# Quantised rows turned by transposing DMA transfers instead of TensorE

## What is computed

```
x = layernorm(x + attention(x, Wq, Wk, Wv, Wo))      # 16 heads of 64, 8 kv heads, rope, tanh cap, causal
scale = max(absmax(x, -1), 1e-7) / 127
q = clip(round(x / scale), -128, 127)                # int8
acc = einsum("bsk,nk->bsn", q, weight)               # the sum in whole numbers
y = float16(acc * scale * w_scale + bias)
out = layernorm(x + y)
```

## Time and profile before

| | |
|---|---|
| median of the three runs | 1320.56 us |
| profiled execution, in all | 1322.9 us |
| its span, first to last instruction | 1321.2 us |
| TensorE busy | 1272.4 us, 96% |
| VectorE busy | 1038.7 us, 79% |
| ScalarE busy | 901.4 us, 68% |
| GpSimd busy | 377.7 us, 29% |
| mean granted TensorE clock | 0.989 |
| DMA, mean rate | 145 GB/s |

### The profile page before, as it was taken

The page is one execution under the profiler, slowest core; times in us unless marked ns, Lnnn a source line. Parts: engine busy times, 40 slices in busy tenths (PEclk is TensorE's granted clock), DMA queues, the critical chain, the costliest instruction groups (busy, mean ns, idle before and its releaser), DMA issues.

```text
span 1321.2 us, 17006 instructions
## 1 busy us (share of the span) xinstructions
PE 1272.4 (96%) x5840; PEld 936.2 (71%) x5840; DVE 1038.7 (79%) x1314; ACT 901.4 (68%) x1019; POOL 377.7 (29%) x438
## 2 busy tenths in 40 slices
PE   6899999999999999999999999999999999999896
PEld 5677777767766777677776777767777677777573
DVE  3588988983679888896478988898556988888566
ACT  4278787862677777875368867687447777879464
POOL 4232231111751111111383111111147211112165
PEclk9899999999999999999999999999999999999898
DMA  9683736495724464748551654466762355353551
GB/s 317 140 280 101 175 113 168 119 243 152 189 69 107 113 149 99 203 92 244 159 152 65 152 112 124 96 184 182 206 185 80 93 139 110 104 116 119 148 142 56
DMA packets 112401, 191.44 MB, mean 145 GB/s; under 512 B 19382, under 2 KB 65980, under 8 KB 104764
## 3 DMA queue, kind: packets, MB, share of 16 engines
q1 hardware_dynamic: 107564, 179.88, 52.1%
q10 hardware_dynamic: 4752, 10.49, 2.1%
HBM read 84.67 MB, written 38.54 MB: 93 GB/s over the span
## 4 chain that ended last, share of the span: by engine, by line
PE 83%; DVE 7%; issue 3%; ACT 3%; DMA 2%; POOL 1%; SPq 1%; POOLq 0%; DVEq 0%; ACTq 0%
PE ps L829 27%; PE ps L749 19%; PE ps L803 17%; PE ps L873 11%; PE ps L770 6%; PE ps L893 1%; PE ps L849 1%; DVE prob_lo L1292 1%; DVE prob_hi L1288 1%; DMA div<-y_scratch 1%; DVE xT L1208 1%; DVE stats L1370 1%; ACT probs L1032 1%; ACT probs L1027 0%; PE ps L883 0%
## 5 line engine op out<-in xcount | busy, mean ns | idle before, releaser
L829 PE MATMUL ps<-prob_hi,v 128*65 128x512 f32 (+3 forms) x1280 | 410.7, 371 | 8.4 <-DVE prob_lo L1292 8.4
L1027 ACT ACTIVATE probs<-ps 128x1024 f32<-128x1024 f32 x288 | 293.6, 1019 | 133.3 <-PE ps L803 133.3
L1292 DVE TENSOR_TENSOR prob_lo<-probs,prob_hi 128x1024 fp32r<-128x1024 f32 x288 | 360.0, 1250 | 9.8
L1535 POOL TENSOR_SCALAR_AFFINE_SELECT probs<-probs 128x256 f32<-128x256 f32 (+1 forms) x192 | 155.6, 818 | 705.3 <-ACT probs L1032 705.3
L803 PE MATMUL ps<-qk 128*128 128x512 f32 (+1 forms) x1280 | 314.5, 372 | 3.0 <-issue 1.8
L1032 ACT ACTIVATE probs<-probs 128x1024 f32<-128x1024 f32 x288 | 305.7, 1061 | 8.6
L749 PE MATMUL ps<-xT,w_ring 128*128 128x512 f32 x1152 | 286.9, 393 | 4.3 <-issue 4.3
L803 PEld LDWEIGHTS ps<-qk 128*128 128x128 f32 x1280 | 224.6, 189 | 62.6 <-issue 3.8
L1288 DVE CAST prob_hi<-probs 128x1024 fp32r<-128x1024 f32 x285 | 203.9, 715 | 79.7 <-POOL probs L1535 48.1
L749 PEld LDWEIGHTS ps<-xT,w_ring 128*128 128x128 f32 x1152 | 215.7, 189 | 50.9 <-issue 5.8
L829 PEld LDWEIGHTS ps<-prob_hi,v 128*65 128x65 f32 (+1 forms) x1280 | 170.7, 135 | 98.7 <-DVE prob_lo L1292 14.6
(11 more groups left out here) (92 smaller groups left out, 964.1 us busy)
## 6 DMA issues: line engine op xcount, KB each, us to landing
qk<-work_r SPq DMA_DIRECT2D x64, 512.0 KB, 8.8
qk<-work_r SPq DMA_DIRECT2D x256, 128.0 KB, 2.7
y_scratch<-sums SPq DMA_DIRECT2D x128, 130.0 KB
y_raw<-y_scratch SPq DMA_DIRECT2D x64, 256.0 KB, 4.3
wo<-wo_scratch SPq DMA_DIRECT2D x7, 2048.0 KB, 8.7
w_ring<-w_scratch SPq DMA_DIRECT2D x12, 1024.0 KB, 6.9
x_raw<-X_T SPq DMA_DIRECT2D x16, 512.0 KB, 6.7
x_in<-X SPq DMA_DIRECT2D x32, 256.0 KB, 4.3
```

The lines of the kernel that those rows point to most:

```text
L829: mm = nc.tensor.matmul(sums_ps[:, :, GQ - w:GQ], v[:, kt, v0:v0 + width], p[:, at, col:col + REP * w].rearrange("p (h q) -> p h q", h=REP ...
L1027: nc.scalar.activation(probs[:, prob_place(g), :], scores[:, g % 2, :], ACT.Tanh, scale=SCORE_SCALE / SOFTCAP).then_inc(capped, 1)
L1292: nc.vector.tensor_tensor(prob_lo[:, prob_place(g), :], probs[:, prob_place(g), :], prob_hi[:, hi_place(g), :].bitcast(F32), ALU.subtract) ...
L1535: nc.gpsimd.affine_select(out=diag, in_=diag, compare_op=ALU.is_ge, fill=0.0, base=0, pattern=[[0, n], [1, P]], channel_multiplier=-1).the ...
```

## The change

The four transposes by the identity on TensorE, the bank they wrote and ScalarE's copy of that bank are gone, with `ident16`. In their place ScalarE issues, right behind the write of `q16`, four DMA transfers that transpose 128 x 128 values of two bytes each from `q16` into `q16T`, of which there are now two, taken in turn, each with its own semaphore. Before issuing, ScalarE waits for its own write, and from tile 2 on for the matmul that read the same `q16T` last. `linear` waits for the four transfers of its tile and, for tile 0, for the copies of the sums that lie in its banks. `quantise` waits for the transfers of the tile before. TensorE's queue has `linear` of tiles 6 and 7 at the same places between the next batch's projections as before.

```diff
-        q16T = over("q16T", "prob_hi", [P, KC, P], BF16, skip=6 * C)
+        q16T = [over("q16T0", "prob_hi", [P, KC, P], BF16, skip=6 * C),
+                over("q16T1", "prob_hi", [P, KC, P], BF16, skip=4 * T + 6 * C)]
...
-        ident16 = sb("ident16", [P, P], BF16)
...
-        q16_ps = ps[:, PV_BANK, 0:C // 2].bitcast(BF16)
...
+        def turned_upto(b, t):
+            return 64 * (b * NT // 2 + t // 2 + 1)
...
@@ TensorE, weigh
-                    if first and (j, c) == (0, 0) and b >= 1:
-                        pe.wait_ge(qT_ready, rows_upto(b - 1, NT - 1))
...
-            def turn_q(b, t):
-                pe.wait_ge(q_done, rows_upto(b, t))
-                if t == 0:
-                    pe.wait_ge(sums_kept, groups_upto(b, NKV - 1, G - 1))
-                for k in range(KC):
-                    mm = nc.tensor.transpose(q16_ps[:, k * P:(k + 1) * P], q16[:, k * P:(k + 1) * P], ident16[:, :])
-                mm.then_inc(q_turned, 1)
-
             def linear(b, t):
-                pe.wait_ge(qT_ready, rows_upto(b, t))
+                pe.wait_ge(q_turned[t % 2], turned_upto(b, t))
                 if t == 0:
                     pe.wait_ge(ffn_cast, 1)
+                    pe.wait_ge(sums_kept, groups_upto(b, NKV - 1, G - 1))
...
-                    mm = nc.tensor.matmul(ffn_ps(b, t), q16T[:, k, :], ffn_wT[:, k, :], start=(k == 0), stop=(k == KC - 1))
+                    mm = nc.tensor.matmul(ffn_ps(b, t), q16T[t % 2][:, k, :], ffn_wT[:, k, :], start=(k == 0), stop=(k == KC - 1))
...
                         linear(b, t - 2)
-                    if t >= 1:
-                        turn_q(b, t - 1)
...
                 if more:
-                    project(m, 0, 8, 20)
-                turn_q(b, NT - 1)
-                if more:
-                    project(m, 0, 20, 24)
+                    project(m, 0, 8, 24)
                 linear(b, NT - 1)
...
@@ ScalarE
                 if t >= 1:
-                    act.wait_ge(q_turned, rows_upto(b, t - 1))
+                    act.wait_ge(q_turned[(t - 1) % 2], turned_upto(b, t - 1))
...
-            def keep_q(b, t):
-                act.wait_ge(q_turned, rows_upto(b, t))
-                nc.scalar.activation(q16T[:, :, :].rearrange("p k n -> p (k n)"), q16_ps, ACT.Copy).then_inc(qT_ready, 1)
+
+            def turn_q(b, t):
+                act.wait_ge(q_done, rows_upto(b, t))
+                if t >= 2:
+                    act.wait_ge(acc_done, rows_upto(b, t - 2))
+                for k in range(KC):
+                    act.dma_start(q16T[t % 2][:, k, :], q16[:, k * P:(k + 1) * P],
+                                  transpose=True).then_inc(q_turned[t % 2], 16)
...
-                    if t >= 2:
-                        keep_q(b, t - 2)
...
                     quantise(b, t - 1)
+                    turn_q(b, t - 1)
                 if more:
                     exponent(b + 1, 0)
-                keep_q(b, NT - 2)
...
                 quantise(b, NT - 1)
+                turn_q(b, NT - 1)
                 if more:
                     cap(b + 1, 1)
                     norm2(b, NT - 3)
-                    keep_q(b, NT - 1)
...
@@ GpSimd, at the start
-            nc.gpsimd.memset(ident16[:, :], 0.0).then_inc(const_zero, 1)
...
-            for i in (ident, ident16):
-                nc.gpsimd.affine_select(out=i[:, :], in_=i[:, :], compare_op=ALU.not_equal, fill=1.0, base=0,
-                                        pattern=[[-1, P]], channel_multiplier=1).then_inc(const_made, 1)
+            nc.gpsimd.affine_select(out=ident[:, :], in_=ident[:, :], compare_op=ALU.not_equal, fill=1.0, base=0,
+                                    pattern=[[-1, P]], channel_multiplier=1).then_inc(const_made, 1)
```

More of the change, by code:

```diff
@@ L283, in attention_block @@
         q_done = sem("q_done")
-        q_turned = sem("q_turned")
-        qT_ready = sem("qT_ready")
+        q_turned = [sem(f"q_turned{n}") for n in range(2)]
         acc_done = sem("acc_done")
@@ L775, in turn_tables @@
             def turn_tables():
-                pe.wait_ge(const_made, 3)
+                pe.wait_ge(const_made, 2)
                 pe.wait_ge(tables_spread, 1)
@@ L1392, in _ @@
             nc.vector.tensor_copy(spread[0:REP, :], spread_f32[0:REP, :]).then_inc(spread_set, 1)
-            dve.wait_ge(const_made, 3)
+            dve.wait_ge(const_made, 2)
             nc.vector.tensor_copy(v[:, :, 0:V_LO].rearrange("p t (j e) -> p t j e", e=VJ)[:, :, :, ONE:VJ],
@@ L1567, in _ @@
             nc.gpsimd.memset(ident[:, :], 0.0).then_inc(const_zero, 1)
-            nc.gpsimd.memset(ident16[:, :], 0.0).then_inc(const_zero, 1)
             nc.gpsimd.memset(one[:, :], 1.0).then_inc(const_made, 1)
             nc.gpsimd.memset(spread_f32[0:REP, :], 1.0).then_inc(const_zero, 1)
-            pool.wait_ge(const_zero, 5)
-            for i in (ident, ident16):
-                nc.gpsimd.affine_select(out=i[:, :], in_=i[:, :], compare_op=ALU.not_equal, fill=1.0, base=0,
-                                        pattern=[[-1, P]], channel_multiplier=1).then_inc(const_made, 1)
+            pool.wait_ge(const_zero, 4)
+            nc.gpsimd.affine_select(out=ident[:, :], in_=ident[:, :], compare_op=ALU.not_equal, fill=1.0, base=0,
+                                    pattern=[[-1, P]], channel_multiplier=1).then_inc(const_made, 1)
             nc.gpsimd.affine_select(out=spread_f32[0:REP, :], in_=spread_f32[0:REP, :], compare_op=ALU.is_ge, fill=0.0,
```

## The result

The changed kernel takes 1424.57 us (median of three runs, 1419.3 to 1426.43) against 1320.56 before: 1.077 times, 95% interval 1.073 to 1.081, slower. The forecast was 1335, range 1315 to 1380; its direction was right and its size was not. The profiled execution is the shortest of the three, 1419.3 us, with a span of 1417.5, against 1321.2 before.

A forecast was written before the change was run, and what follows sets the result against it. TensorE, busy 96% of the span, was taken as the bound. 8.3 us at three seam ends, 1.05 in the last seam and 5.1 for the clock made +14.4, 1337.3 on the profiled execution, so 1335 us; range 1315 to 1380.

The forecast's parts named there:

- I = 0.60: Time for ScalarE to issue one transposing DMA, taken as 0.60 us, with ends 0.338 and 1.222.
- rival B: ScalarE becomes the bound in the seams: 1355 us at 0.80 per issue, 1398 at 1.222; chance 0.17.
- H: Hold of ScalarE's queue per tile, the wait for the write plus four issues: 2.45 us, ends 1.4 and 4.9.
- T: Time from a tile's quantised write until all four transfers have landed: 4.55 us, ends 3.1 and 6.4.
- clock 1.7: Loss to TensorE's lowered clock after its stall at a seam's end: 1.7 us for each of three seams, +5.1.
- its landing is hidden too: In a seam's middle the landing costs nothing, as `linear` wants the row more than a tile later.
- most of the gain: Removing TensorE's transposes gains 1.95 us per seam: five times 0.31 plus 0.40 at tile 0.
- the path through the seam's end: Tile 6's hold passes through exponent, mask, inverse deviation, norm1 and quantise to tile 7; net +2.77 us per seam, +8.3 for three.
- The gap of about 5 us: TensorE stands idle about 5.3 us before tile 7's `linear` in three seams.
- C of the prediction: The four transposes don't overlap, each landing 2.1 us after the one before: 1351 us; chance 0.13.
- D: Short issues and landings, and VectorE catching up during the stall behind the seams, make the kernel faster: 1313 us; chance 0.22.
- E: The transfers go as element-sized pieces and not as a hardware transpose: far over 1400 us; chance 0.03.

The follow-up runs named there:

- alone: A kernel that computes nothing and makes transposing and plain DMAs of several sizes on an idle core; 1.10 us per issue for 128 columns.
- plain_aside: The kernel before, plus four plain 128x128 DMAs per tile on ScalarE into a buffer nobody reads; 1361.91 us, 1.031 times.
- sp_four: The changed kernel with its four transposing DMAs per tile issued by SyncE, behind its loads, in place of ScalarE; 1378.4 us, 1.0425 times.
- one_dma: The changed kernel with one transposing DMA of 128x512 per tile in place of four of 128x128; 1336.46 us, 1.0115 times.
- late_weights: The changed kernel with SyncE's two weight loads of a seam moved from row tile 1 to row tile 4; 1417.32 us, 1.072 times.
- one_late_exp: As one_late, with tile 6's transposing DMA issued behind the next batch's first exponent in place of ahead of it; 1315.34 us, 0.9954 times.
- one_late: As one_dma, with SyncE's two weight loads of a seam issued at row tile 4 in place of 1; 1327.81 us, 1.0051 times.
- late_after: As one_late, with SyncE's 512 KB load for the next batch waiting until tile 7 has landed transposed; 1321.85 us, 0.9992 times.

## Why the prediction missed

**The step that failed is the length of one issue.** It took I = 0.60 from SyncE's plain puts of 128 KB, "nearest" since a transpose writes many short pieces. The pieces are short, as the page of after shows (39862 DMA packets under 512 B, 19382 before), but the length of the issue doesn't follow from them. A transposing DMA takes 1.265 in the kernel and 1.10 with nothing else running, a plain one 0.47 (128x512, alone) to 0.62 (128x128, plain_aside). The upper end, 1.222 from the 512 KB puts, agrees with the measured length by accident: a transposing DMA is that long with 4 KB as with 128 (16x128 and 128x512 in alone). The ends were kept, but the range was cut at 1380, inside rival B.

**It was rival B.** "From I = 0.64 on, round and hold pass 7.11 and each tile of a seam pays": shown by the round of 9.31 us, where 6.95 was forecast, by sp_four and one_dma. B had a chance of 0.17 and a price of 1398 at I = 1.222. With the measured sizes its sum is: middle 5 x (9.30 - 7.42) = 9.4 a seam; end, with H = 0.05 + 4 x 1.265 = 5.11 and T = 0.05 + 3 x 1.265 + 2.6 = 6.45, 5.11 + 6.45 - 2.28 = 9.3; clock 1.7; together 20.4 three times, and 9.4 + 6.45 - 1.36 = 14.5 in the last: +76.

**What the sum had at nothing.** Measured are +96 on the span. The missing 20 are about 7 in each of three seams and 4.4 in the last, less the 3.8 us of scatter ahead of the first seam and about 1 between seams. The 7 are as large as the waits for the late first landing (8.2, 6.9 and 6.7 us): "so there its landing is hidden too" was said of the middle and taken for the first tile as well, and `quantise`'s wait for the transfers of the tile before, 12.6 us in three waits, had no term at all. The first tile's transposes hold ScalarE's queue from 330.1, SyncE's loads for the seam are issued from 332.6 to 334.7, and the DMA engines are full. In the first seam they land 5.3 to 9.9 us after their issue, those of tiles 4 to 6 2.2 to 2.9, and tile 7's 2.2 to 4.5. First the changed kernel, then the kernel before at the place of the same loads (columns as in the earlier trace rows):

```profile
340.00:348.00 8.00, 3.70 (x8) 1.88 (x10) 1.94 (x4) 0.72 (x1) 2.62 (x4) 0.50 1.06 252
```

```profile
338.00:342.00 4.00, 4.00 (x21) 2.78 (x20) 1.76 (x5) 2.34 (x4) 2.40 (x1) 1.00 1.00 207
342.00:346.00 4.00, 4.00 (x18) 3.07 (x17) 3.22 (x8) 2.46 (x4) 3.05 (x4) 1.00 1.06 370
```

In the changed kernel TensorE's clock is at 0.50 (1.2 GHz of 2.4) behind the stall. By late_weights the loads at row tile 1 are the cause of most of the first wait. The prediction read the DMA engines only as a mean over the seam, 0.49; the shares of 1.00 and 1.06 stood in the trace of before, and nobody waited for them there.

**What held.** Direction; most of the gain, since with the hold small the tiles are 7.19 apart (one_dma), 0.23 less than before, where the sum had 0.31; the landing of 2.7 (measured 2.6 in the median of the changed kernel) except at the start of a seam; the path through the seam's end: in the changed kernel the exponent starts 5.06 us behind tile 6's write and norm1 of tile 7 behind that, and with one DMA instead of four one_late_exp took the 1.4 us away that it held them; the low clock behind the stall. The gap of about 5 us in front of tile 7's `linear` came true by luck (5.02, 5.96 and 5.92): H + T - 1.7 gives 9.9 us with the measured sizes, and the gap is smaller because TensorE itself, held up tile by tile, comes there late. C of the prediction, that the landings come one after another, is out: away from the loads they land 2.2 to 2.9 after their own issue. D is out too: `weigh`'s waits for VectorE fell only from 8.4 to 5.5 us. And E is out.

**The rule weighed.** The issue measured 1.10 to 1.30 us, time of the issuing queue, and the landing comes 2.2 us or more after the issue's start. The Trainium skill, "VectorE: DVE Perf Modes", section "The three transpose paths", gives 1309 ns for a 128x128 transpose by DMA; the measured issue is near it and the landing is not. The Trainium skill, "Advanced Engine Details and Errata", section "X-Bar Transpose (TRN2)", calls transposing DMAs "as fast as regular DMAs". In alone that holds about for the landing, 2.4 us against 2.0 for a tile of 128x512, and not for the issue, 1.21 against 0.47. The prediction gave the first rule a time of 1344, because it put the 1.3 us into T alone; put into the hold H as well, it is rival B a little past its upper end.

**What stays open.** What the change would cost if an issue were truly 0.60; why a transposing issue is as long as it is; and the last seam, which measured 18.9 us where the sum gives 14.5: TensorE waits 7.52 us there for tile 6 too, which the sum had not priced.

## What to carry to other kernels

Before moving work to a DMA, price the instruction that issues it, by its kind: on the engine's queue it is held time like any other, and a price borrowed from another kind of DMA is not a bound. Where it is dear and doesn't grow with size, send one for the whole tile (1424.6 to 1336.5 us here), and put it behind what the next engine waits for. Then look, around each new transfer on which someone waits, at what the other queues issue within some microseconds of it: of the 15.9 us that were left, 8.7 and 6.0 went when two loads were moved or made to wait, and the first of these moves brought at most 7.3 us, not clear of noise, as long as ScalarE had no slack for it.

## What the runs showed of the hardware

- A transposing DMA holds its queue, on ScalarE and on SyncE, for 1.09 to 1.11 us at 16x128 to 128x128, 1.19 to 1.21 at 128x512, and 1.27 to 1.30 behind another one (alone); at the start of a seam, with the DMA engines full, up to 2.43 (the changed kernel). A plain copy of 128x512 takes 0.47.
- It lands 2.2 to 2.4 us after the issue's start with the DMA engines idle (alone), 4.5 when a load of 512 KB is issued in the same moment (one_late), and up to 9.9 in the changed kernel and 10.3 in sp_four beside the loads of a seam. Plain DMAs of 128x128 too land up to 8.1 us after their issue there (plain_aside).
- One DMA with `transpose=True` from 128x512 into 128x4x128 does what four of 128x128 do, for one issue of 1.21 us (one_dma).
- Four plain DMAs of 128x128, a hold of 2.43 us a tile on an engine that was busy 68% of the span, cost 40 us in the kernel before, the waits for their landing and for the copy behind them included.
- A wait of 2.76 us of TensorE left its granted clock at 1.00 (late_after); one of 5.03 at the same place was followed by 0.50 (one_late).
